# A chunked gated delta rule on one core: norms kept in reading order, a weights load that waits for another landing, and a new order of the stages

## What is computed

```
qkvz = x @ W_qkvz                          # 16 key heads; each: q, k (128), v (2 x 128), z (2 x 128)
q, k, v = silu(causal conv of 4 taps)      # along the tokens
q, k = q / |q|, k / |k|                    # the norms of the change are those of k
per value head (32) and chunk:             # chunks in order
    attn = tril(q k^T * decay)
    T = inverse(1 + tril(k_beta k^T * decay, -1))
    vn = T v_beta - (T k_beta exp(g)) state
    out = (q exp(g)) state + attn vn
    state = state * exp(g_last) + (k exp(g_last - g))^T vn
x = out * silu(z); x = x / rms(x) * norm_weight; y = x @ W_out
```

## Time and profile before

| | |
|---|---|
| runs, us | 4620.41, 4631.10, 4628.52; median 4628.52 |
| the profiled execution: its own time, its span | 4659.61 us, 4657.8 us |
| mean granted PE clock | 0.979 |
| PE busy | 4215.2 us (90%) |
| PEld busy | 3757.0 us (81%) |
| ACT busy | 3830.0 us (82%) |
| DVE busy | 3657.7 us (79%) |
| POOL busy | 2368.6 us (51%) |
| HBM traffic | 125 GB/s over the span, 38.9% of the time of 16 DMA engines |

### The profile page before, as it was taken

The page is one execution under the profiler, slowest core; times in us unless marked ns, Lnnn a source line. Parts: engine busy times, 40 slices in busy tenths (PEclk is TensorE's granted clock), DMA queues, the critical chain, the costliest instruction groups (busy, mean ns, idle before and its releaser), DMA issues. The chain is left out here.

```text
span 4657.8 us, 139558 instructions
## 1 busy us (share of the span) xinstructions
PE 4215.2 (90%) x44242; PEld 3757.0 (81%) x44242; DVE 3657.7 (79%) x6626; ACT 3830.0 (82%) x10831; POOL 2368.6 (51%) x3362
## 2 busy tenths in 40 slices
PE   3399999999999999999999999999999999999497
PEld 2288888888888888888888888888888888888476
DVE  4288888888888888888888888888888888888454
ACT  1388888888898888988889888898898988888244
POOL 4355555555545555455555555555555555555244
PEclk9699999999999999999999999999999999999799
DMA  6544443433434344343343443433434434343000
GB/s 196 187 138 125 130 140 122 138 125 130 143 122 134 125 129 144 121 134 128 127 144 124 131 133 123 143 123 132 134 123 142 125 130 139 121 140 107 32 14 23
DMA packets 365392, 584.77 MB, mean 126 GB/s; under 512 B 148240, under 2 KB 228624, under 8 KB 347920
## 3 DMA queue, kind: packets, MB, share of 16 engines
q1 hardware_dynamic: 364560, 583.70, 38.9%
q10 hardware_dynamic: 768, 0.26, 0.0%
HBM read 533.81 MB, written 50.07 MB: 125 GB/s over the span
## 5 line engine op out<-in xcount | busy, mean ns | idle before, releaser
L924 DVE SCALAR_TENSOR_TENSOR conv<-ps,cws,conv 128x511 f32<-128x511 f32 (+2 forms) x1536 | 1084.9, 741 | 68.2 <-ACT conv L812 56.8
L1116 POOL TENSOR_TENSOR xo<-xo,zs 128x512 f32<-128x512 f32 x256 | 326.3, 1275 | 1559.5 <-DVE xo L1018 1559.5
L630 PE MATMUL ps<-xb,wb 128*128 128x512 f32 x3072 | 841.1, 409 | 76.9 <-DMA wb<-w_scratch 73.3
L630 PEld LDWEIGHTS ps<-xb,wb 128*128 128x128 f32 x3072 | 541.8, 190 | 169.8 <-issue 73.5
L967 DVE CAST_PREDICATED pl<-masks,ps 128x512 f16<-128x512 uint16 x768 | 544.7, 709 | 56.2 <-PE ps L692 32.5
L873 ACT ACTIVATE t<-ps 128x512 f16<-128x512 f32 x768 | 465.3, 606 | 119.3 <-PE ps L700 108.5
L877 ACT ACTIVATE u<-ps 128x512 f16<-128x512 f32 x768 | 463.5, 604 | 43.7 <-PE ps L705 43.7
L790 PE MATMUL ps<-wo,xt 128*128 128x256 f32 x3072 | 427.9, 289 | 25.3 <-issue 23.4
L644 PE MATMUL ps<-wb,xb 128*128 128x256 f32 x3072 | 430.1, 290 | 0.0
L812 ACT ACTIVATE conv<-ps,cws 128x512 f32<-128x512 f32 x512 | 360.0, 703 | 69.7 <-PE ps L630 61.5
L790 PEld LDWEIGHTS ps<-wo,xt 128*128 128x128 f32 x3072 | 382.5, 189 | 39.4 <-issue 34.5
(11 more groups left out here) (158 smaller groups left out, 11557.9 us busy)
## 6 DMA issues: line engine op xcount, KB each, us to landing
xb<-x_scratch SPq DMA_DIRECT2D x128, 1024.0 KB, 5.9
wb<-w_scratch SPq DMA_DIRECT2D x128, 1024.0 KB, 7.5
grow<-rows_scratch SPq DMA_DIRECT2D x128, 512.0 KB, 3.7
wb<-w_scratch SPq DMA_DIRECT2D x128, 512.0 KB, 4.2
wo<-wout_scratch SPq DMA_DIRECT2D x128, 512.0 KB, 6.2
rk<-rk_scratch SPq DMA_DIRECT2D x128, 256.0 KB, 5.5
w_scratch<-wsplit SPq DMA_DIRECT2D x128, 192.0 KB, 3.4
wpiece<-in_Wqkvz SPq DMA_DIRECT2D x128, 96.0 KB, 2.1
```

Of the source, the lines that this page charges most:

```text
L630: last = nc.tensor.matmul(proj_bank[c][:, :], wb[:, pw, k * WCOL + c * D:k * WCOL + (c + 1) * D], xb[p][:, px, k * S:(k + 1) * S], start=( ...
L924: nc.vector.scalar_tensor_tensor(out=conv[c][:, back:S], in0=proj_bank[c][:, 0:S - back], scalar=cws[p][:, c * TAPS + 3 - back:c * TAPS + ...
L1116: nc.gpsimd.tensor_tensor(x, x, zs[p][:, 2 * g:2 * g + 2, :, :], ALU.mult).then_inc(gated.sem, 1)
```

## The change

Three edits. First, the row of norms is written chunk first, token last ("reading order"), so that `keys` reads `rk` densely; the store now scatters single numbers of 4 bytes. Second, `load_w` waits, beside the wait that it had, until the row load of the item before has landed (`rk_in`). Third, `ORDER` is new, with offsets from -3 to 2 in place of -2 to 3, and with it the banks of nine groups of stages and the waits that guard them. No stage is added or dropped, and none does other work. Rounds run from -2 to 130 in place of -3 to 129, and the loop holds rounds 6 to 125, 120 as before.

In the diff a line of "..." stands for the old list, which is in the kernel above.

```diff
--- before.py
+++ after.py
@@ -427,12 +427,12 @@
         y_bank, o_bank, p_bank, t_bank, u_bank = ps[0], ps[1], ps[2], ps[3], ps[4]
         ks_at, upd_at, qs_at = y_bank[:, 0:R * D], y_bank[:, R * D:2 * R * D], o_bank[:, 0:R * D]
         resid_bank, fix_bank = (u_bank, t_bank), (p_bank, u_bank)
-        proj_bank = (ps[5], ps[6], ps[5], ps[6])
-        z_bank = (ps[5], ps[6])
-        turn_bank = (ps[7], ps[5], ps[7], ps[5])
-        gram_bank = (ps[6], ps[7])
-        o_turn_bank = (ps[7], ps[7])
-        out_bank = (ps[7], ps[7])
+        proj_bank = (ps[7], ps[6], ps[5], ps[6])
+        z_bank = (ps[5], ps[5])
+        turn_bank = (ps[7], ps[7], ps[7], ps[7])
+        gram_bank = (ps[5], ps[6])
+        o_turn_bank = (ps[5], ps[6])
+        out_bank = (ps[7], ps[5])
 
         w_dst = wb[:, :, :].bitcast(f32).rearrange("p q (k n) -> p (q k) n", k=KT)
 
@@ -511,34 +511,36 @@
         g0, g1 = 0, 1
         K, Q, V0, V1 = range(4)
         ORDER = (
-            at(1, ("taps", 0)) + at(0, ("t_first", g0), ("diagonal", g1), ("rounded", g1), ("u_first", g1), ("z", g1)) + at(-2, ("o_norm", g1))
...
+            at(0, ("conv", K, 3)) + at(1, ("taps", 0)) + at(-1, ("z", g1)) + at(-3, ("o_rnorm", g1)) + at(-1, ("p", 0), ("turn", V0))
+            + at(-3, ("o_turn", g0)) + at(-1, ("t_mm", 0), ("silu", V1), ("u_mm", 0), ("vt", 0)) + at(-2, ("residual", 1)) + at(0, ("conv", Q, 3))
+            + at(-3, ("x_copy", g0)) + at(-2, ("y", 1)) + at(-3, ("x_low", g0)) + at(-1, ("t_copy", 0)) + at(-3, ("o_norm", g1))
+            + at(-1, ("u_copy", 0), ("turn", V1)) + at(0, ("silu", K)) + at(-3, ("o_turn", g1)) + at(-1, ("p_mm", 1)) + at(-2, ("out", 0))
+            + at(-3, ("x_copy", g1)) + at(0, ("project", V0)) + at(-1, ("vt", 1), ("p", 1), ("t_mm", 1)) + at(-2, ("qs_mm", 1), ("y_copy", 1))
+            + at(-3, ("x_low", g1)) + at(-2, ("update_mm", 1)) + at(-1, ("t_copy", 1), ("p_mm", 2), ("u_mm", 1)) + at(-2, ("state", 1))
+            + at(0, ("turn", K)) + at(-1, ("p", 2)) + at(-2, ("ks_mm", 2), ("q_part", 1), ("residual", 2)) + at(-1, ("rnorm", Q))
+            + at(-2, ("intra_mm", 1)) + at(-1, ("kw", 0)) + at(-2, ("out", 1)) + at(0, ("tap", V0)) + at(-1, ("u_copy", 1)) + at(0, ("squares", K),
+               ("conv", V0, 1)) + at(-1, ("t_mm", 2)) + at(0, ("project", V1)) + at(-1, ("t_copy", 2)) + at(1, ("mask_row", g0))
+            + at(-1, ("p_mm", 3)) + at(0, ("key_tokens", 0)) + at(-1, ("u_mm", 2)) + at(0, ("tap", V1)) + at(-2, ("y", 2)) + at(-1, ("u_copy", 2))
+            + at(-2, ("qs_mm", 2), ("y_copy", 2)) + at(-1, ("low", g0), ("p", 3)) + at(0, ("conv", V1, 1)) + at(-2, ("q_part", 2))
+            + at(-1, ("t_mm", 3)) + at(0, ("rnorm", K), ("store_norm", 0), ("load_norm", 0)) + at(1, ("load_w", 0)) + at(0, ("conv", V0, 2))
+            + at(-1, ("u_mm", 3)) + at(0, ("conv", V1, 2)) + at(-2, ("update_mm", 2)) + at(-1, ("t_copy", 3)) + at(-2, ("intra_mm", 2), ("gate", g0))
+            + at(-1, ("p_mm", 4)) + at(-2, ("state", 2)) + at(-3, ("out_mm", g0)) + at(-2, ("o_square", g0)) + at(-1, ("u_copy", 3))
+            + at(-2, ("o_rnorm", g0)) + at(-1, ("p", 4), ("low", g1), ("t_mm", 4), ("t_copy", 4)) + at(1, ("split", 0), ("store_split", 0))
+            + at(2, ("load_raw", 0)) + at(-2, ("ks_mm", 3), ("out", 2), ("qs_mm", 3)) + at(-3, ("added", g0)) + at(0, ("silu", Q))
+            + at(-2, ("residual", 3)) + at(-1, ("p_mm", 5), ("u_mm", 4), ("u_copy", 4)) + at(-2, ("y", 3)) + at(-1, ("p", 5)) + at(-2, ("q_part", 3))
+            + at(0, ("turn", Q)) + at(-1, ("t_mm", 5)) + at(-2, ("y_copy", 3)) + at(-1, ("u_mm", 5)) + at(0, ("conv", V0, 3)) + at(-1, ("t_copy", 5),
+               ("u_copy", 5)) + at(0, ("keys", 0)) + at(-2, ("intra_mm", 3)) + at(0, ("conv", V1, 3), ("gram", g0), ("system", g0))
+            + at(-1, ("resid_mm", g0)) + at(0, ("squares", Q), ("attn", g0)) + at(-1, ("resid", g0), ("resid_mm", g1), ("resid", g1))
+            + at(0, ("gram", g1), ("system", g1)) + at(-3, ("out_mm", g1)) + at(-2, ("load_wout", 0)) + at(-1, ("fix_mm", g0))
+            + at(0, ("diagonal", g0), ("attn", g1)) + at(-1, ("fix_mm", g1), ("fix", g0)) + at(0, ("silu", V0)) + at(-1, ("fix", g1))
+            + at(1, ("decay", g0)) + at(-1, ("residual", 0)) + at(-3, ("added", g1)) + at(0, ("rounded", g0)) + at(1, ("mask_row", g1))
+            + at(0, ("diagonal", g1)) + at(-2, ("out", 3)) + at(1, ("project", K), ("project", Q)) + at(0, ("rounded", g1)) + at(1, ("decay", g1))
+            + at(2, ("load_rows", 0)) + at(-1, ("y", 0)) + at(0, ("u_first", g0)) + at(1, ("tap", K), ("tap", Q)) + at(0, ("project_z", g0))
+            + at(-1, ("y_copy", 0), ("intra_mm", 0)) + at(1, ("conv", K, 1)) + at(-2, ("gate", g1)) + at(0, ("t_first", g0)) + at(1, ("conv", Q, 1))
+            + at(0, ("u_first", g1), ("small", 0), ("z", g0)) + at(1, ("conv", K, 2)) + at(0, ("t_first", g1)) + at(-1, ("update_mm", 0))
+            + at(0, ("project_z", g1)) + at(1, ("load_wz", 0)) + at(2, ("load_x", 0)) + at(1, ("conv", Q, 2)) + at(0, ("t_first_copy", 1),
+               ("t_first_copy", 0)) + at(-2, ("o_square", g1)) + at(-1, ("state", 0)) + at(-2, ("o_norm", g0)) + at(0, ("p_mm", 0))
+            + at(-1, ("ks_mm", 1))
         )
         FAR, NEAR = max(o for o, *_ in ORDER), min(o for o, *_ in ORDER)
         LOOP = 2 * ((3 - NEAR) // 2), 2 * ((ITS - FAR) // 2)
@@ -566,6 +568,7 @@
 
             def load_w(a, p, _):
                 proj_mm.wait(sp, a - 1, 4)
+                rk_in.wait(sp, a - 1, 16)
                 sp.dma_start(w_dst[:, :, 0:S], w_dram[ds(a // B, 1)].rearrange("a p q n -> p (a q) n")[:, :, 0:S]).then_inc(w_in.sem, 16)
 
             def load_wz(a, p, _):
@@ -595,7 +598,7 @@
             def store_norm(a, p, _):
                 sp.wait_ge(rnorm.sem, rnorm.at(a, 1))
                 rk_in.wait(sp, a - 1, 16)
-                sp.dma_start(rk_dram[0].rearrange("(i n) -> i n", n=NC), rn[:, :]).then_inc(rk_out.sem, 16)
+                sp.dma_start(rk_dram[0].rearrange("(n i) -> i n", n=NC), rn[:, :], allow_slow_non_contiguous=True).then_inc(rk_out.sem, 16)
 
             def load_norm(a, p, _):
                 sp.wait_ge(rk_out.sem, rk_out.at(a, 16))
@@ -619,13 +622,13 @@
                     pe.wait_ge(w_in.sem, w_in.at(a, 16))
                     pe.wait_ge(x_in[p].sem, x_in[p].at(a // 2, 16))
                 if c == K:
-                    z_ready.wait(pe, a - 1, 1)
+                    squares.wait(pe, a - 1, 2)
                 if c == Q:
-                    z_ready.wait(pe, a - 1, 2)
+                    attn_ready.wait(pe, a - 1, 2)
                 if c == V0:
-                    vt_ready.wait(pe, a - 1, 2) or tapped.wait(pe, a, convolved(K))
+                    xt_low.wait(pe, a - 3, 1) or z_ready.wait(pe, a - 1, 2)
                 if c == V1:
-                    tapped.wait(pe, a, convolved(Q))
+                    xt_low.wait(pe, a - 3, 2) or tapped.wait(pe, a, convolved(Q))
                 for i, (k, pw, px) in enumerate(PASSES):
                     last = nc.tensor.matmul(proj_bank[c][:, :], wb[:, pw, k * WCOL + c * D:k * WCOL + (c + 1) * D],
                                             xb[p][:, px, k * S:(k + 1) * S], start=(i == 0), stop=(i == len(PASSES) - 1))
@@ -635,9 +638,9 @@
                 if g == 0:
                     pe.wait_ge(wz_in.sem, wz_in.at(a, 16))
                 if g == g0:
-                    squares.wait(pe, a, 2)
+                    added.wait(pe, a - 3, 2) or attn_ready.wait(pe, a, 1)
                 if g == g1:
-                    attn_ready.wait(pe, a, 1)
+                    z_ready.wait(pe, a, 1)
                 for n in range(2):
                     for i, (k, pw, px) in enumerate(PASSES):
                         at = k * S + (2 * g + n) * C
@@ -649,13 +652,13 @@
             def turn(a, p, c):
                 pe.wait_ge(silued.sem, silued.at(a, c + 1))
                 if c == K:
-                    added.wait(pe, a - 3, 2) or vt_ready.wait(pe, a - 1, 1)
+                    vt_ready.wait(pe, a - 1, 2)
                 if c == Q:
-                    tapped.wait(pe, a, convolved(V0))
+                    added.wait(pe, a - 3, 1) or keys_copied.wait(pe, a, 1)
                 if c == V0:
-                    xt_low.wait(pe, a - 2, 2) or attn_ready.wait(pe, a, 2)
+                    tapped.wait(pe, a + 1, convolved(K)) or squares.wait(pe, a, 2)
                 if c == V1:
-                    tapped.wait(pe, a + 1, convolved(K)) or z_ready.wait(pe, a, 1)
+                    vt_ready.wait(pe, a, 1)
                 for n in range(NC):
                     src = kq[p][:, n, 1, :] if c == Q else conv[c][:, n * C:(n + 1) * C]
                     last = nc.tensor.transpose(turn_bank[c][:, n * C:(n + 1) * C], src, ident[:, :])
@@ -665,9 +668,9 @@
                 pe.wait_ge(kq_ready.sem, kq_ready.at(a, 1))
                 pe.wait_ge(silued.sem, silued.at(a, Q + 1))
                 if g == g0:
+                    tapped.wait(pe, a, convolved(V0))
```

(30 more changed lines are left out.)

6 lines of the change are left out of this document (removed).

## The result

The changed kernel takes 5522.58 us (median of 4 runs) against 4629.81 for the kernel before on the same chip: 1.193 times, 95% interval 1.191 to 1.195. Its profiled execution took 5524.69 us, its span is 5522.9. The forecast was 4510, the range ended at 4660.

What follows compares the result with a forecast made beforehand. PE was taken as the bound, with a wait before gram: 32.29 - 1.26 + .3 = 31.3 us a round, 123 less over 128 items plus 5 for filling, so 4628.5 - 118 = 4510; range 4455 to 4660.

Steps and rivals of the forecast that it cites:

- What bounds the kernel: PE bounds the loop, busy 30.83 of 32.29 us a round; one wait before gram, 1.26, is nearly all it loses.
- one circle only, through the weights: From project K through store, row and weights to the next project K: 30.4 us, bounds 29.6 and 33.0, in time.
- e: How much later the store of norms lands as 512 pieces of 4 bytes: 0 to 2.0 us, taken .5.
- The price of a packet: In the store of norms, 8.7 ns a packet; four times as many packets add .2 us.
- the nearest store by count: Store of the split weights, also 512 packets: lands after 2.4 us, 3.4 in the loop, against 1.4 for the norms.
- The held weights: Holding load_w until the row lands gives the row's load .5 us, bounds 0 and 2.4.
- The order by the keys and by the weights: Before gram .3 us of wait stays, bounds 0 and 2.5; weights reach project K in time by .6 to .9.
- the sum: A round of 31.3 us; over 128 items 123 less, plus 5, so 118 less than before: 4510.
- the read: The dense multiply in keys takes .68 us instead of 1.075, shortening the wait before gram.
- the order's small waits: Elsewhere in the new order, places with .1 to .3 us to spare, none stalling PE; bounds -.45 and +1.0, taken +.0.
- filling and draining: The first and last rounds lose part of 17 us as an item takes longer: bounds 0 and 17, taken 5.
- C: Rival: weights come late to project K, .7 us a round at the upper end, 4720 in all; chance .17.

Runs made afterwards that it cites:

- before_two_stores: Kernel before with a second store like the first (128 pieces of 16 bytes) issued ahead of it and waited for: 5014.50 against 4655.18, 1.076.
- pieces_8: Changed kernel with the row stored as 256 pieces of 8 bytes and keys reading with a step of two: 4607.40 us, 0.996 of the kernel before.
- second run of stores: Kernel before with stores of 4-byte pieces in other patterns ahead of its item loop, each waited for; runs of sixteen took 6.7, 3.4 and 4.8 us.
- row_only: Kernel before with the row in reading order and nothing else: 5947.07 against 4667.90, 1.274.

## Why the prediction was wrong, point by point

- **What bounds the kernel.** Right that one wait before `gram` was nearly all that PE lost. But I took PE's work for the bound, with a wait in it. It was a circle, and it comes out of the trace of before:
```profile
2009.66 1.99 PE L673 MATMUL ps<-kq 128*128 128x256 f32 x8 [0.54 <-DVE kq L933]
...
2030.50 0.63 PE L661 MATMUL ps<-ident,conv 128*128 128x128 f32 x4
```
From `gram` to the end of K's transpose, in the next item's turn, 21.2 us of PE, 1.4 on ACT, 1.5 on POOL, 7.1 from the store to `keys`, 1.2 to `gram`: 32.4, and the round was 32.29. In such a circle each us of the store is a us of the round, at the least, and `before_two_stores` shows it: 1.4 us gave 3.0. I drew one circle only, through the weights.
- **The store: the step that failed.** "So the landing comes e later, with e from 0 to 2.0 ... I take e = .5." In the changed kernel's loop the load is issued 8.2 us after the store in the median, 8.6 in the mean, so e is 6.8. The price of a packet, 8.7 ns, was right (7.6), and tells nothing of the arrival. The split weights, "the nearest store by count", had pieces of 384 bytes: the count was not the thing that two stores must share. The rule of the Trainium skill that I set against the row (DMA: Bandwidth & Descriptors, Rules for kernel authors, one descriptor for each element, rearrange it away) had the better advice; that each number becomes a piece of its own agrees (528 packets in the queue), but the count doesn't make the price: 512 pieces of 4 bytes apart land after 2.1 to 2.6, 128 side by side after 7.6 to 8.7.
- **The held weights.** ".5 us, not more" was wrong: 1.4 or 1.5 in the three pairs of kernels that differ in them (5.5 to 4.1 twice, 6.2 to 4.7). I had read 49 GB/s as a sign that the weights did not share the queue with the row, and the last item's 5.0, which has another load behind it, as the row alone. The row alone takes 3.0 to 3.3, or 4.1 fresh after its store.
- **The order by the keys and by the weights.** With the upper e, I had `gram` late by up to 2.5 and the circle of the weights at 33.0. With e = 6.8 the circle through `gram` is, in the new order, 19.7 on PE, 1.4, 1.5, 12.8 from store to `keys` (2023.59 to 2036.41) and .8 to `gram`: 36.2. The clock, for which the prediction had no term, adds 2.3: 38.5. Some .6 is left of 39.13; the mean store is later than this round's by .7. (The upper bound 33.0 of the weights' circle is a slip: its terms add up to 32.8.)
- **The rest.** With the store undone the round is 31.21, where the sum said 31.3, and 0.970 of the kernel before; 4510 would have been 0.974. So the read (.69), the order's small waits, filling and draining were sized well enough together, and that is in part luck: the held weights and the small waits erred in opposite senses, and with the read strided the new order has 31.6.
- **The rivals.** C had the right sign and the wrong place: `project` K waits 5.6 us in 119 rounds for its weights. It "decides from a circle of 32.3 on", that is from a store later by 1.3 to 2.4, and it was later by 6.8; I gave it .17 for want of a row that showed a store of such pieces. The 32.3 is where the time would grow, not where the weights begin to cost: by the prediction's own terms their circle is 31.5 with a store 1.6 later, already over the 31.2 that the kernel reaches with the store undone, and `pieces_8`, with such a store, waits for them .5 us a round. In the changed kernel the wait before `gram` holds PE back so long that the weights are there.

Not settled: why the arrival depends on the neighbourhood as it does in the second run of stores, and why the same store takes 9.0 us in the old order and 8.2 in the changed kernel (8.7 there without the held weights).

## What to carry to other kernels

When a change touches a transfer that some engine waits for, look for every circle that it closes from round to round (here two, through `gram` and through the weights), and put its arrival, not its packets, into the sum; if no row shows a transfer of the same pattern, measure it alone before laying an order around it. Don't scatter single numbers side by side into HBM: keep a partition's numbers together and pay the stride where they are read (here .4 us, against 7). A load that many wait for should go ahead of a large one with its landing awaited, which was worth 2.0% to 2.7% in the old order and nothing in the new.

## What the runs showed of the hardware that I had not expected

- Stores of 2 KB or less to HBM took from 1.4 to 10.0 us by their pattern, where the packets of the two stores of norms took 8.7 and 7.6 ns each: 128 pieces of 4 bytes side by side up to 8.7, 64 bytes apart 1.4.
- A row read by all partitions just after its store landed one us later than when read again (4.1 against 3.0), and 1.6 later after the store of 4-byte pieces (4.9 against 3.3).
- A wait of 5.2 us on PE took the granted clock from 1.00 to 0.50, and it stayed there for some 4 us of work. So a late transfer can cost more than its delay: 3.0 us a round for a store 1.4 later (`before_two_stores`), 10.2 for one 7.6 later (`row_only`).
